# One fused kernel, its attention stage: r blocks copied an eighth later, and two of eight exponentials made wide behind a GpSimd subtraction

## The reference, cut to what matters

```python
q = conv1x1(wq, x).reshape(n, NH, HD, H, W)      # k, v alike; n 4, NH 16, HD 16, H = W = 128
qk  = einsum('nhcij,nhciw->nhijw', q, k) / D
qrq = einsum('nhcij,chjw->nhijw', q, rq) / D
krk = einsum('nhcij,chjw->nhijw', k, rk) / D
weight = softmax(qk + Gq * qrq + Gk * krk, axis=3)
out = einsum('nhijw,nhciw->nhcij', weight, Gv1 * v) + einsum('nhijw,chjw->nhcij', weight, Gv2 * rv)
```

## Time and profile before

| | us |
|---|---|
| median of 3 runs | 7508.54 (7497.94 to 7526.4) |
| the profiled execution | 7515.16 |
| its span in the trace | 7513.4 |
| project and before | until some 1500 |
| attend | some 1500 to 5890 |
| combine, experts | from there to the end |

### The profile page before, as it was taken

How to read it: one execution, slowest core, us unless ns; L and a number is a source line. 1 busy time by engine, 2 the same in 40 slices (tenths; PEclk the granted TensorE clock), 3 DMA queues, 4 the chain that set the end, 5 groups by cost and what they waited for, 6 DMA issues and landing times. The chain is left out here.

```text
span 7513.4 us, 279833 instructions
## 1 busy us (share of the span) xinstructions
PE 6392.3 (85%) x106442; PEld 4983.2 (66%) x106442; DVE 5358.7 (71%) x20905; ACT 4722.5 (63%) x11171; POOL 2483.9 (33%) x1267
## 2 busy tenths in 40 slices
PE   4999999979989999889998999989999766576558
PEld 3555555568878888788887888878888433232258
DVE  5444444448878888788887888878888788898820
ACT  0444444358988888888888888888888334333300
POOL 0000000025545545445544454444544322232110
PEclk7999999969999999999999999999999988898755
DMA  7555555557677677767777677767766667686422
GB/s 217 202 205 206 206 205 205 180 89 125 122 130 128 117 130 130 123 117 128 127 121 129 119 124 130 126 121 121 134 120 116 207 228 231 193 264 196 143 96 95
DMA packets 1197409, 1146.43 MB, mean 153 GB/s; under 512 B 625632, under 2 KB 956000, under 8 KB 1194144
## 3 DMA queue, kind: packets, MB, share of 16 engines
q1 hardware_dynamic: 1006816, 842.59, 54.1%
q10 hardware_dynamic: 188352, 285.27, 10.3%
q0 software_dynamic: 1024, 2.09, 0.1%
HBM read 708.04 MB, written 421.56 MB: 150 GB/s over the span
## 5 line engine op out<-in xcount | busy, mean ns | idle before, releaser
L790 POOL TENSOR_TENSOR att_scores<-att_scores,att_inverse 128x1024 f32<-128x1024 f32 x1024 | 1993.8, 1949 | 2139.3 <-DVE att_inverse L738 2138.8
L697 ACT ACTIVATE att_scores<-att_scores,att_negmax 128x128 f32<-128x128 f32 x8192 | 2515.0, 394 | 26.1 <-issue 20.8
L753 DVE CUSTOM_DVE_ANT_0 att_scores<-att_ps,att_scores 128x128 f32<-128x128 f32 x8192 | 1817.8, 289 | 831.9 <-PE att_ps L614 803.0
L603 PE MATMUL att_ps<-att_qk,att_rs 32*128 32x64 f32 x32768 | 2174.1, 280 | 80.5 <-DMA att_qk<-qk 38.7
L614 PE MATMUL att_ps<-att_own 32*128 32x128 f32 x16384 | 1811.2, 322 | 338.0 <-ACT att_scores L690 166.4
L603 PEld LDWEIGHTS att_ps<-att_qk,att_rs 32*128 32x128 f32 x32768 | 2022.5, 195 | 88.0 <-issue 81.3
L614 PEld LDWEIGHTS att_ps<-att_own 32*128 32x128 f32 x16384 | 1595.2, 197 | 654.5 <-issue 334.0
L656 PE MATMUL att_ps<-att_scores,att_rv 128*16 128x64 f32 x32768 | 1391.0, 331 | 18.7 <-issue 16.6
L736 DVE TENSOR_REDUCE att_total<-att_scores 128x8 f32<-128x1024 f32 x1024 | 1241.4, 1212 | 0.0
L690 ACT ACTIVATE att_scores<-att_ps 128x1024 f32<-128x1024 f32 x1024 | 1032.5, 1008 | 323.7 <-PE att_ps L603 322.4
L656 PEld LDWEIGHTS att_ps<-att_scores,att_rv 128*16 128x16 f32 x32768 | 1129.8, 119 | 41.3 <-issue 31.1
(11 more groups left out here) (147 smaller groups left out, 5072.9 us busy)
## 6 DMA issues: line engine op xcount, KB each, us to landing
qk<-proj_qk_out ACTq DMA_DIRECT2D x64, 2048.0 KB, 8.6
att_qk<-qk SPq DMA_DIRECT2D x512, 256.0 KB, 5.9
att_own<-qk SPq DMA_DIRECT2D x1024, 128.0 KB, 4.3
proj_x<-in_x_dram SPq DMA_DIRECT2D x128, 512.0 KB, 4.3
v_t<-proj_v_out ACTq DMA_DIRECT2D x64, 1024.0 KB, 11.4
att_vt<-v_t SPq DMA_DIRECT2D x256, 256.0 KB, 5.2
att_v<-att_att_v SPq DMA_DIRECT2D x1024, 64.0 KB, 3.7
att_r<-att_att_r SPq DMA_DIRECT2D x1024, 64.0 KB, 2.6
```

Source lines behind the costliest of these rows:

```text
L603: return pe.matmul(ps[:, 4 + gg, jj * IU:(jj + 1) * IU], rs[32 * g:32 * g + 32, j, :], qk[v % 2][32 * g:32 * g + 32, :, j, :], start=True, ...
L697: last = act.activation(scores[v % BUFS][:, i, :], scores[v % BUFS][:, i, :], ACT.Exp, bias=negmax[v % BUFS][:, i:i + 1], scale=-1.0)
L753: last = dve.tensor_tensor_reduce(out=scores[v][:, i, :], in0=ps[:, 2 * (p % 2) + r // HR, (r % HR) * W:(r % HR + 1) * W], in1=scores[v][: ...
L790: pool.tensor_tensor(piece(scores[v], p), piece(scores[v], p), piece(inverse[v], p).unsqueeze(3).broadcast_to([P, 2, HR, W]), ALU.mult).th ...
```

## The change

ScalarE copies a block of r sums in the eighth after the one in which it did (b = 1 in eighth 0, 2 in 2, 3 in 4, and 0 in eighth 6), between the two halves of that eighth's exponentials and not behind the relative copy. For pieces 0 and 4 of each unit GpSimd subtracts the negated maxima from the scores (`shift`), and ScalarE takes one exponential of 128 x 1024 elements two eighths behind the piece (in eighths 2 and 6, behind the exponentials of pieces 1 and 5), in place of 8 of 128 x 128 one eighth behind it. VectorE's sums of pieces 0 and 4 move one eighth back with it, just ahead of those of pieces 1 and 5: eighths 2 and 6 have no sums, 3 and 7 have two. GpSimd's order is written anew, with the last two pieces of a unit normalised behind the first subtraction of the next, and the third and fourth quarters of the tables scaled one place earlier among the pieces than they were.

```diff
+SHIFTED = (0, 4)
...
+            def exp_shifted(u, v, p):
+                act.wait_ge(shifted, len(SHIFTED) * u + SHIFTED.index(p) + 1)
+                act.activation(piece(scores[v % BUFS], p), piece(scores[v % BUFS], p), ACT.Exp, scale=-1.0).then_inc(exped, 2)
...
                 for p in range(PIECES):
-                    if p == 0:
-                        if back1:
-                            exp_half(u - 1, v - 1, HALVES - 2)
-                            exp_half(u - 1, v - 1, HALVES - 1)
-                    elif now:
-                        exp_half(u, v, 2 * p - 2)
-                        exp_half(u, v, 2 * p - 1)
+                    for half in range(2):
+                        if p == 0 and back1:
+                            exp_half(u - 1, v - 1, HALVES - 2 + half)
+                        if p and now and p - 1 not in SHIFTED:
+                            exp_half(u, v, 2 * p - 2 + half)
+                        if half == 0 and p % 2 == 0 and p < 6 and back2:
+                            read_r(u - 2, 1 + p // 2)
+                        if half == 0 and p == 6 and back1:
+                            read_r(u - 1, 0)
+                    if now and p - 2 in SHIFTED:
+                        exp_shifted(u, v, p - 2)
                     if p < 6 and ahead1:
                         read_relative(u + 1, v + 1, p + 2)
                     if p >= 6 and ahead2:
                         read_relative(u + 2, v + 2, p - 6)
-                    if p % 2 and p < 4 and back2:
-                        read_r(u - 2, 2 + p // 2)
-                    if p % 2 and p >= 4 and back1:
-                        read_r(u - 1, p // 2 - 2)
...
-                dve.wait_ge(exped, HALVES * u + 2 * k + 2)
+                dve.wait_ge(exped, HALVES * u + 2 * k + (4 if k in SHIFTED else 2))
...
-                    if k >= 0 and now:
+                    if k >= 0 and now and k not in SHIFTED:
+                        if k - 1 in SHIFTED:
+                            sums_of(u, v, k - 1)
                         sums_of(u, v, k)
...
+            def shift(u, v, p):
+                pool.wait_ge(added, HALVES * u + 2 * p + 2)
+                pool.tensor_tensor(piece(scores[v], p), piece(scores[v], p), piece(negmax[v], p).unsqueeze(3).broadcast_to([P, 2, HR, W]),
+                                   ALU.subtract).then_inc(shifted, 1)
...
-            def head(h, last):
+            def head(h, first, last):
                 for k in range(UPH):
-                    for p in range(PIECES):
-                        if k == UPH - 2 and not last and p % 2 == 1:
-                            scale_relative(h + 1, p // 2)
-                        normalise(UPH * h + k, k % BUFS, p)
+                    u, v = UPH * h + k, k % BUFS
+                    fresh = k == UPH - 2 and not last
+                    shift(u, v, 0)
+                    if k or not first:
+                        normalise(u - 1, (k - 1) % BUFS, 6)
+                        normalise(u - 1, (k - 1) % BUFS, 7)
+                    normalise(u, v, 0)
+                    if fresh:
+                        scale_relative(h + 1, 0)
+                    normalise(u, v, 1)
+                    shift(u, v, 4)
+                    normalise(u, v, 2)
+                    if fresh:
+                        scale_relative(h + 1, 1)
+                    normalise(u, v, 3)
+                    normalise(u, v, 4)
+                    if fresh:
+                        scale_relative(h + 1, 2)
+                    normalise(u, v, 5)
+                    if fresh:
+                        scale_relative(h + 1, 3)
...
```

More of the change, by code:

```diff
@@ L428, in attend @@
         v_done, r_done, v_read, r_read = (s.sem(n) for n in ("v_done", "r_done", "v_read", "r_read"))
-        cleared = s.sem("cleared")
+        cleared, shifted = s.sem("cleared"), s.sem("shifted")
         v_stored = [s.sem(f"v_stored{a}") for a in range(2)]
@@ L791, in normalise @@
                                    ALU.mult).then_inc(normed, 1)
-            def head(h, last):
-                for k in range(UPH):
-                    for p in range(PIECES):
-                        if k == UPH - 2 and not last and p % 2 == 1:
-                            scale_relative(h + 1, p // 2)
-                        normalise(UPH * h + k, k % BUFS, p)
+            def shift(u, v, p):
[3 more added lines that the diff above has]
+            def head(h, first, last):
+                for k in range(UPH):
+                    u, v = UPH * h + k, k % BUFS
[19 more added lines that the diff above has]
+                        scale_relative(h + 1, 3)
             for a in range(QUARTERS):
                 scale_relative(0, a)
-            with pool.Fori(0, NH - 1) as h:
-                head(h, False)
-            head(NH - 1, True)
+            head(0, True, False)
+            with pool.Fori(1, NH - 1) as h:
+                head(h, False, False)
+            head(NH - 1, False, True)
+            normalise(UNITS - 1, (UNITS - 1) % BUFS, 6)
+            normalise(UNITS - 1, (UNITS - 1) % BUFS, 7)
 def combine(nc, d):
```

## The result

The changed kernel takes 7553.88 us (median of 6 runs, 7539.47 to 7562.45) against 7505.82 for the one before (6 runs, 7497.09 to 7526.4): ratio 1.0066, interval 1.005 to 1.0083. It is slower, by 48 us. I had forecast slower, by 206; the sign held and the size did not.

What follows compares the result with a forecast made beforehand. ScalarE and TensorE were taken to hold each other through the r copy. Loop +212, clock +102, short stalls -64 and head's end -45 gave +205 on 7515.2, 7714 at the median; own range 7600 to 7800, 8 in 10 7510 to 7840.

Steps and rivals of the forecast that it cites:

- The loop (+212): Attend: VectorE's and ScalarE's work in series makes a half-unit 16.29 us against 15.46, +212 us for the stage.
- both bunches: VectorE's work in eighths 3 and 7 (5.28 us) and ScalarE's in 2 and 6 (4.7), standing in series.
- The other marks named in advance: VectorE idle 2.3 us before pieces 3 and 7, ScalarE waiting 1.1, quiet unit 32 to 34, clock below 0.96.
- The r copy and TensorE's floor: Attend: moving the r copy removes ScalarE's 0.6 us wait and alone leaves TensorE's 29.3 us a unit.
- rival 1: Attend: the bunches do not meet and units run at TensorE's floor, gaining 205 us, about 7305; faster side 14%.
- TensorE's clock (+102): Attend: gaps before eighths 3 and 7 lower TensorE's clock half the time, 0.8 us each time, +102 us.
- The head's end (-45): End of each head: slower units shorten the wait from SyncE's backlog by about 3 us, 15 times, -45 us.
- shift(0) comes late behind the fourth quarter of the tables: Head's end: the last unit's subtraction would end near 2890 and delay eighth 3 by about 5 us.
- ScalarE's wait for the subtraction: Attend: GpSimd's subtraction was to cost 0, bound +1 us a unit; ScalarE waiting for it would show the forecast wrong.
- under cover of the wait for `own`: Head's end: the wait for `own` hides the late subtraction; without it the cost is up to 75 us.
- The short stalls (-64): Attend: TensorE's idle time absorbs 4 of some 7 us of short stalls a head, -64 us.
- Rival 2: Attend: loop only 16.0 us a half-unit, no clock penalty, stalls absorb it; about 7510 to 7540 us; 11%.

Runs made afterwards that it cites:

- e4: The changed kernel with the wide exponential moved behind the relative copy in eighths 2 and 6, double sums kept; ratio 0.9987 to the kernel before.
- e5: The changed kernel with VectorE's sums three eighths behind each piece, one piece in each eighth; ratio 0.9972 to the kernel before.
- e1: The kernel before with only the r copies moved into the next eighth's exponentials; 7436.8 us, ratio 0.9923.
- e12: The changed kernel with GpSimd's scaling of the tables' fourth quarter behind the subtraction of piece 0 in a head's last unit; ratio 1.0092 to the kernel before.

## Why the prediction was wrong in size

The measured 7554 lies inside the range for 8 in 10 (7510 to 7840) and below the forecast's own range (7600 to 7800). The mechanism of the slower loop was right. Two terms failed, each by over 60 us and both the same way: the price of TensorE's clock and what the head's end gives back.

**The loop (+212).** Right in every member and nearly in its sum: 0.73 a half-unit, +187. The wide exponential took 1.00 from start to start (I took 0.95), the two sums 2.82 (2.98). e4 and e5 show both bunches in it. TensorE's idle time came as one wait of some 1.5 in front of eighths 3 and 7, not as 1.2 there and 0.4 before eighths 2 and 6. The other marks named in advance are there: VectorE idle 2.33 before the adds of pieces 3 and 7, ScalarE waiting 0.88 for adds (1.1 expected), a quiet unit of 32.4, and a granted clock of 0.95 from 2500 to 3500 us (0.96 before).

**The r copy and TensorE's floor.** Right in quiet running (29.2 a unit in e1). But I let that floor stand for rival 1's gain of 205, with the stalls unchanged, and repeated it in the expectation of e1: the run gave a quarter of it, since only a third of its half-units run at the floor.

**TensorE's clock (+102).** This step failed in its price. Behind 22 gaps of 1.45 to 1.64 us in front of eighths 3 and 7 (2430 to 3170 us) the mean granted clock of the next 6 us was lower 8 times, and behind 109 gaps of 1.2 to 1.8 from 1910 to 5600 us 45 times: 41%, not far from the half that I took. (The trace of the kernel before has 23 gaps of 0.7 to 1.4 us between 1900 and 3600 us, not 20 as the prediction says, 10 of them with a lower clock behind.) Two of the windows (PE busy, granted clock):

```profile
2574.85:2580.85 6.00, 6.00 (x135) 0.72 0.35 83
3016.09:3022.09 6.00, 6.00 (x160) 1.00 0.56 88
```

But a lower stretch cost less than the 0.8 that I took. From the timeline of the changed kernel:

```profile
2574.85 0.38 PE L615 MATMUL att_ps<-att_own 32*128 32x128 f32 x1 [1.63 <-ACT att_scores L691]
2591.43 0.38 PE L615 MATMUL att_ps<-att_own 32*128 32x128 f32 x1 [0.89 <-ACT att_scores L691]
```

That half-unit took 16.58, 0.39 over a quiet one. 0.39 x 8 / 22 x 256 makes some 36 us, an estimate from one such pair. Over the stage, the 41 half-units that can be followed behind a gap with a lower clock took 16.55 at the median, and 57 behind the other gaps 16.28: 0.27 x 0.41 x 256 = 28 us. Both are estimates; no run takes the clock's effect out by itself.

**The head's end (-45).** The mechanism was right and the term mis-sized, and this the runs without tables show: 11.2 and 4.0 a head, so -108. I had set it at 3 us by how much slower the last units run, but TensorE's wait for `own` nearly vanished, from 121 to 10 us between 1910 and 5600 us. The chain that it waits for hardly depends on the loop: from SyncE's first issue of a head's tables until `own` of the last unit has landed, the traces have 47.7 us before and 46.3 in the changed kernel (medians of 14 heads), although a unit of the changed kernel is 1.5 us longer. A slower TensorE thus comes to it later and waits less. The quiet units alone make some 3 us of that, as I had it; how the other 4 a head divide no run shows. That shift(0) comes late behind the fourth quarter of the tables was right, and that quarter alone moved (the third stands between the same pieces as before, contrary to the section on the change). But I put ScalarE's wait for the subtraction at nothing, under cover of the wait for `own`, and named such a wait as a sign of being wrong. It came once a head, 1.0 to 4.1 us long and 38 us in all, since the cover went. e12 shows that it is hardly paid on top: without it TensorE waits for `own` instead.

```profile
3182.13 1.06 ACT L703 ACTIVATE att_scores<-att_scores 128x1024 f32<-128x1024 f32 x1 [4.01 <-POOL att_scores L802]
```

**The short stalls (-64).** Without tables the stalls are 10.2 and 8.3 a head, -30 with the clock's price in it; with that price at 36 the absorption is about 66, as taken, and with 28 it is 58. This split is worked out, not shown.

Together: 187 - 108 - 30 = +49, and 48 was measured. My +205 had the clock some 66 too high, the head's end 63 too small and the loop 25 too high. The sign held because the loop's +187 is more than all that came back. Rival 2, a small loss by absorption (7510 to 7540), was the nearest to the outcome; I gave it 11%. It had the head's end at 45 like the forecast.

## What to carry to other kernels

Balance is per turn of the loop, not per unit of work: two pieces of work that are each within the bottleneck's time make a new bound when one order puts them in series. Write down the chain from one turn of the bottleneck to the next, term by term, before trusting sums of busy time; here it was right to 0.1 us. Then ask what the stalls between quiet turns wait for: a chain that does not depend on the loop (here the loads at a head's end) takes back part of a loss. It need not swallow a gain: that of the r copy alone went in the short stalls. An experiment that removes such a chain shows most of the loop's worth (here 154 of 187 us).

## What I had not expected

- A wait of about 1.5 us by TensorE, between the r sums of one eighth and the own scores of the next, left the clock at 2.4 GHz 14 times in 22, and in the half-unit followed here, where it fell to 1.2, the time grew by only 0.39 us.
- TensorE's waits for nothing visible grew from 90 to 140 us when only ScalarE's order changed (e1), and shrank to 59 in the changed kernel, where TensorE has idle time of its own. In these three kernels, the quicker the loop, the more of them show.
- The wide exponential had a mean of 1120 ns where the relative copy of as many elements had 1016.
